# Perceiver kernel: queries stored from ScalarE's queue, the first pair's keys fetched beside the last projection blocks, the negated maxima rounded by ScalarE

## The reference, cut to what matters

```python
# layer 0, cross-attention: 16 heads of 16 channels, all masks true
xn = (x - mean(x)) / sqrt(var(x) + 1e-5)
q = (xn @ Wq + bq)          # (2, 256, 256)
k = (ctx @ Wk + bk)         # (2, 4096, 256)
v = (ctx @ Wv + bv)
p = softmax(q_h @ k_h.T / sqrt(16))   # per head h
x = x + concat_h(p @ v_h) @ Wo + bo
```

## Time and profile before

| | us |
|---|---|
| runs, median of 3 | 1144.29 (1140.45 to 1147.24) |
| the profiled execution | 1140.79 |
| its span, first to last instruction | 1139.5 |
| projection, to the barrier | 0 to 140.7 |
| first attention | 140.7 to about 534 |
| the rest (not touched) | about 534 to 1139.5 |

### The profile page before, as it was taken

One profiled execution on the slowest core, in us unless ns is written; L12 is line 12 of the kernel. 1 busy time (PEld: TensorE's weight loads), 2 busy tenths in 40 slices (PEclk: granted clock), 3 DMA queues, 4 the chain that ended last, 5 costly groups with the idle time before them and its releaser, 6 DMA issues. The chain is left out here.

```text
span 1139.5 us, 20829 instructions
## 1 busy us (share of the span) xinstructions
PE 955.4 (84%) x7631; PEld 599.1 (53%) x7648; DVE 848.7 (74%) x1772; ACT 651.4 (57%) x1067; POOL 295.7 (26%) x313
## 2 busy tenths in 40 slices
PE   5997859999999999996989989248878888987586
PEld 5876724444444444443668875134555556634354
DVE  5775789999899999942567876998878785265447
ACT  3442307788788888874445425059999997202121
POOL 1000088899600000000112521006373631000010
PEclk9999958999999999997789996567799989997797
DMA  5867642222222222200312228002363136830000
GB/s 178 310 234 272 239 134 61 76 79 83 76 74 79 81 79 77 74 1 12 103 49 77 71 61 221 1 1 60 97 181 87 56 98 209 203 110 1 1 1 19
DMA packets 99322, 111.83 MB, mean 98 GB/s; under 512 B 26658, under 2 KB 75731, under 8 KB 99219
## 3 DMA queue, kind: packets, MB, share of 16 engines
q1 hardware_dynamic: 96802, 109.50, 32.0%
q10 hardware_dynamic: 2416, 0.99, 0.4%
HBM read 80.95 MB, written 29.43 MB: 97 GB/s over the span
## 5 line engine op out<-in xcount | busy, mean ns | idle before, releaser
L835 ACT ACTIVATE pT<-bank 128x512 f32<-128x512 f32 x512 | 278.5, 597 | 93.2 <-PE bank L752 71.9
L857 DVE TENSOR_REDUCE rmax<-bank 128x2 f32<-128x1024 f32 x256 | 307.3, 1223 | 26.4 <-PE bank L720 25.4
L764 PE MATMUL bank<-pT,V 128*17 128x256 f32 x2048 | 161.1, 387 | 4.7 <-ACT oT L841 4.5
L1679 PE MATMUL bank<-K1s,qs 97*128 97x512 f32 x256 | 116.7, 558 | 54.7 <-ACT below L1788 36.7
L752 PEld LDWEIGHTS bank<-qs,ks 49*128 49x128 f32 x1024 | 77.7, 186 | 112.4 <-ACT pT L835 98.9
L1943 POOL TENSOR_TENSOR total<-total,work 128x1024 f32<-128x1024 f32 x40 | 94.8, 2378 | 159.0 <-ACT work L1797 158.1
L752 PE MATMUL bank<-qs,ks 49*128 49x256 f32 x1024 | 130.0, 332 | 2.3 <-ACT pT L835 0.5
L720 PE MATMUL bank<-ks,qs 49*128 49x512 f32 x512 | 110.6, 427 | 16.2 <-DMA ks<-k_parts_d 9.0
L1679 PEld LDWEIGHTS bank<-K1s,qs 97*128 97x128 f32 x256 | 54.8, 227 | 69.8 <-ACT below L1788 38.0
L1849 DVE MAX8 cand<-work 128x8 f32<-128x128 f32 x384 | 76.4, 278 | 0.0
L764 PEld LDWEIGHTS bank<-pT,V 128*17 128x17 f32 x2048 | 34.5, 95 | 63.2 <-ACT pT L835 44.7
(11 more groups left out here) (452 smaller groups left out, 1841.6 us busy)
## 6 DMA issues: line engine op xcount, KB each, us to landing
k_parts_d<-kparts SPq DMA_DIRECT2D x48, 512.0 KB
ks<-k_parts_d SPq DMA_DIRECT2D x381, 64.0 KB, 2.2
K1s<-k_parts_d SPq DMA_DIRECT2D x96, 128.0 KB
cn<-in_ctx SPq DMA_DIRECT2D x32, 384.0 KB, 4.0
cx<-in_ctx SPq DMA_DIRECT2D x16, 384.0 KB, 5.0
w<-in_L_ffn_w SPq DMA_DIRECT2D x32, 128.0 KB, 2.7
w2e<-in_L_ffn_w SPq DMA_DIRECT2D x16, 128.0 KB, 2.4
W<-in_L_xattn_W SPq DMA_DIRECT2D x2, 1024.0 KB, 8.3
```

The source lines that it names most:

```text
L764: t = pe.matmul(bank[32 * c:32 * c + VW, 7, a * S:(a + 1) * S], V[:, b * NCH + 4 * g + c, h, :], pT[:, (at + 2 * (c // 2) + a) % 8, c % 2 ...
L835: p_made.up(act.activation(pT[:, at % 8, :], bank[:, 4 + at % 3, :], ACT.Exp))
L857: max_read.up(dve.tensor_reduce(rmax[p % 2][:, :, qt, c], bank[:, b0:b0 + 2, :], AX.X, ALU.max))
L1679: m = pe.matmul(bank[:, b0 + c, :], qs1[0:NROW1, b * H1 + h, q], K1s[h][0:NROW1, keys], start=True, stop=(what == "new"))
```

## The change

Three edits.

1. **Queries stored from ScalarE's queue.** The twelve stores leave `keys_sync`. `keys_scalar` issues three after the last key part of block 8, three after block 9, and two after each of blocks 10, 11 and 12.
2. **The first pair's keys and queries are fetched in the projection.** A third key buffer `kf` and the query buffers `qs` are allocated before the projection: `kf` where `Ap` lies later, `qs` behind `Bp`. ScalarE's program issues the rows of ones after block 10, the keys of the pair's first head after block 13 (three DMAs of 256 KB) and of its second head after block 14, then waits for the query stores and issues the queries of pairs 0 and 1 (four DMAs of 49 KB). After the barrier SyncE starts with the keys of pair 1 and goes on with pair 2 without a wait; ScalarE issues two rows of ones for each of the two buffers `ks`. Pair 0 computes from `kf`. GpSimd's powers wait, before they write `Ap` and `Bp`, until pair 0 is scored.
3. **The negated maxima are rounded by ScalarE.** `copy_rows` moves from `heads_vector` to `heads_scalar`, with its own count `rows_read`; for pair `p+1` it stands before unit 25 of pair `p`, between the two `Exp` of step 12, for pair 0 before all units. Waits for a max bank go through `read_by`, which picks `rows_read` or `max_read`.

```diff
     V = sb("V", [P, NB * NCH, H0, VW])
+    HALF_P = P // 2
+    below = spot[0]
+    spot[0] = LATER + 2 * 4 * LB * 32 * 4
+    qs = [sb(f"qs{j}", [P, S], F32R) for j in range(3)]
+    spot[0] = END - 2 * S2 * 4
+    kf = sb("kf", [P, S2], F32R)
+    spot[0] = below
...
-            if n in (8, 9):
-                store_queries(n - 8)
...
+    def store_queries(mt, b, k):
+        act.wait_ge(*q_split.at(2 * mt + 2))
+        h0 = b * H0 + mt * (P // D0)
+        r0, kp, qp = STACK[k]
+        q_stored.up(act.dma_start(q_stack_d[h0:h0 + P // D0, r0:r0 + D0, :], qparts[:, mt, qp, b * S:(b + 1) * S].bitcast(F32)), 16)
+
+    def load_queries(queue, p):
+        for a in range(2):
+            query_in[p % 3].up(queue.dma_start(qs[p % 3][HALF_P * a:HALF_P * a + NROW, :].bitcast(F32), q_stack_d[2 * p + a]), 16)
+
+    def key_ones(queue, keys, done):
+        for a in range(2):
+            r = HALF_P * a + MAX_ROW
+            done.up(queue.dma_start(keys[r:r + 1, :].rearrange("p (a n) -> p a n", a=8).bitcast(F32),
+                                    ones[0:1, :].rearrange("p (a n) -> p a n", a=1).to_broadcast([1, 8, 512])), 16)
+
+    def load_first_keys(a):
+        for r0, kp, qp in STACK:
+            kf_in.up(act.dma_start(kf[HALF_P * a + r0:HALF_P * a + r0 + D0, :].bitcast(F32),
+                                   k_parts_d[a * D0:(a + 1) * D0, kp, :]), 16)
...
# keys_scalar, at the end of each block n
+            if n in (8, 9):
+                for k in range(NSTK):
+                    store_queries(0, n - 8, k)
+            if n in (10, 11, 12):
+                for b in range(2):
+                    store_queries(1, b, n - 10)
+            if n == 10:
+                key_ones(act, kf, kf_in)
+            if n in (13, 14):
+                load_first_keys(n - 13)
+            if n == 14:
+                act.wait_ge(*q_stored.at(16 * (1 + 4 * NSTK)))
+                load_queries(act, 0)
+                load_queries(act, 1)
...
+    def read_by(at):
+        rows = sum(what[1] == "rows" for what in passing[:at + 1])
+        return rows_read.at(rows) if passing[at][1] == "rows" else max_read.at(at + 1 - rows)
+
+    def keys_of(p):
+        return ks[p % 2] if p else kf
...
# powers_pool, before the first write of Ap
+        pool.wait_ge(*st_made.at(UNITS))
...
     def heads_sync():
+        for p in range(1, NP_):
             if p >= 3:
                 sp.wait_ge(*st_made.at(UNITS * (p - 2)))
             if p >= 2:
+                load_queries(sp, p)
             for q in range(4):
+                if p >= 3:
+                    sp.wait_ge(*st_made.at(UNITS * (p - 2) + 8 * (q + 1)))
+                for a in range(2):
+                    load_key_parts(sp, p, a, q)
...
# heads_tensor: max_step, turn_rows, add_quarters
-                pe.wait_ge(*max_read.at(at - 1))
+                pe.wait_ge(*read_by(at - 2))
# scores
-                pe.wait_ge(*max_read.at(place[p, "rows"] + 1))
+                pe.wait_ge(*rows_read.at(p + 1))
...
     def heads_scalar():
+        for j in (1, 0):
+            key_ones(act, ks[j], kones_in[j])
+
+        def copy_rows(p):
+            at = place[p, "rows"]
+            act.wait_ge(*max_made.at(at + 1))
             for a in range(2):
                 r = HALF_P * a + MAX_ROW
+                t = act.copy(qs[p % 3][r:r + 1, :], bank[r:r + 1, 2 * (at % 2), 0:S])
+            rows_read.up(t)
...
+        copy_rows(0)
         for p in range(NP_):
             for u in range(UNITS):
+                if u == 2 * (16 - LEAD) + 3 and p + 1 < NP_:
+                    copy_rows(p + 1)
                 exps(p, u)
...
# heads_vector: copy_rows is gone, "rows" is passed over
```

More of the change, by code:

```diff
@@ L300, in build @@
     V = sb("V", [P, NB * NCH, H0, VW])
+    HALF_P = P // 2
[5 more added lines that the diff above has]
+    spot[0] = below
+    kf_in = flag("kf_in")
+    query_in = [flag(f"query_in{j}") for j in range(3)]
     phase_begins()
@@ L542, in build @@
     phase_ends()
[L545 removed]
+    NP_ = NH // 2
     G = 8
@@ L567, in build @@
     key_in = [[flag(f"key_in{j}{q}") for q in range(4)] for j in range(2)]
-    query_in = [flag(f"query_in{j}") for j in range(3)]
-    max_made, max_read, nmax_made = (flag(n) for n in ("max_made", "max_read", "nmax_made"))
+    max_made, max_read, rows_read, nmax_made = (flag(n) for n in ("max_made", "max_read", "rows_read", "nmax_made"))
     st_made, p_made, pv_made, oT_copied, den_made, o_done = (flag(n) for n in (
@@ L751, in scores @@
                     rows = slice(HALF_P * a, HALF_P * a + NROW)
-                    t = pe.matmul(bank[:, 4 + (at + a) % 3, c * S:(c + 1) * S], ks[p % 2][rows, k0:k0 + P],
+                    t = pe.matmul(bank[:, 4 + (at + a) % 3, c * S:(c + 1) * S], keys_of(p)[rows, k0:k0 + P],
                                   qs[p % 3][rows, :], start=True, stop=True)
@@ L858, in max_step @@
             if u == 15:
-                dve.wait_ge(*max_read.at(at + 1))
+                dve.wait_ge(*read_by(at))
                 nmax_made.up(dve.tensor_reduce(nmax[:, :, :].rearrange("p t (a m) -> p a t m", a=2)[:, :, :, MAX_ROW],
                                                rmax[p % 2][:, :, :, :], AX.X, ALU.max, negate=True))
-        def copy_rows(p):
-            at = place[p, "rows"]
-            dve.wait_ge(*max_made.at(at + 1))
-            for a in range(2):
-                r = HALF_P * a + MAX_ROW
-                t = dve.tensor_copy(qs[p % 3][r:r + 1, :], bank[r:r + 1, 2 * (at % 2), 0:S])
-            max_read.up(t)
         def take_sums(p):
@@ L877, in divide @@
             pairs = slice(b * H0 // 2, (b + 1) * H0 // 2)
-            dve.wait_ge(*max_read.at(place[pairs.stop - 1, "sums"] + 1))
+            dve.wait_ge(*read_by(place[pairs.stop - 1, "sums"]))
             if b == 0:
@@ L911, in heads_vector @@
                     add_batch(0)
-            else:
+            elif u != "rows":
                 max_step(p, u)
```

55 lines of the change are left out of this document (13 added, 42 removed).

## The result

Six runs of the changed kernel have the median 1157.01 us (1154.49 to 1160.3), the kernel before 1140.81 us on the same chip: ratio 1.0132, 95% interval 1.0101 to 1.0162. The forecast of 1141.3 us was wrong: 16 us slower instead of 3 us faster. The profiled execution took 1157.37 us, with a span of 1156.1 against 1139.5.

The account below looks back on a forecast made before the run. It took TensorE as the projection's bound except for waits, and TensorE with the score matmul and `Exp` ring just below in attention. Terms -4.6 - 4.0 + 2.0 + 3.6 = -3.0 us gave 1141.3 us, range 1133.5 to 1149.

Parts of the forecast that it names:

- query stores: Projection, blocks 9 and 10: context loads issued earlier, TensorE's waits of 5.6 us shrink, gain 4.6 us.
- first keys, behind the barrier: After the barrier: first max matmul no longer waits for key loads, 4.0 us less, bounds 0 and 4.1.
- barrier later for the fetch: End of projection: early loads delay the last stores and move the barrier by 2.0 us, bounds 0 and 4.
- rounding, 15 pairs: First attention: copies on ScalarE cost net 0.24 us a pair, 15 times, 3.6 us more.
- remaining waits: Projection: TensorE's waits for context loads left after moving the query stores, put at 1.0 us, between 0 and 5.6.
- rival D: Projection: context loads land as late as before because the DMA bytes are the same; 1145.9 us, chance 0.17.
- 0.99 MB at 346 / 0.89 = 389 GB/s are 2.5 us, of which about 0.5 us fits between the stores: Before the barrier: DMA time of the loads after block 14, moving the barrier by 2.0 us.
- The far bound of 4 us: Barrier's largest delay: loads to 16 partitions at half the rate, none fitting between the stores.
- with 256 columns ... 0.27 us, both 0.54: Step 12 on ScalarE: time of the two rounding copies, interpolated from 128-partition copies of 128 and 512 columns.
- the same ring: First attention: score matmul, `Exp`, next score matmul; a late `Exp` delays step 14's score matmul, by 0.30 us.
- C: First attention: copies between `Exp`s cost 0.78 us per pair, 11.7 in all; 1149.4 us, chance 0.13.
- Rival B: First attention: the rounding copies hide in ScalarE's slack; 1136.8 us, chance 0.25.

Follow-up runs that it names:

- e2: Kernel before with query stores and rounding on ScalarE, without the early fetch of keys and queries: 1149.86 us, ratio 1.0065.
- e5: Kernel before with only the query stores moved to ScalarE's queue: 1139.02 us, ratio 0.9976.
- e3: Changed kernel with the rounding copies one unit earlier, ahead of unit 24, where ScalarE is idle: 1144.97 us, ratio 1.0027.
- e11: Changed kernel with 24 early 64 KB key loads from SyncE after blocks 10 to 13, rounding back on VectorE: 1137.50 us, ratio 0.9944.
- e10: Changed kernel with rounding back on VectorE and two unread 128x256 float32 copies in its place on ScalarE: 1141.70 us, run once.
- e8: Changed kernel with 24 early 64 KB key loads from SyncE after blocks 10 to 13, rounding on ScalarE ahead of unit 24: 1137.14 us, ratio 0.9967.
- e6: Kernel before with only the rounding moved to ScalarE, ahead of unit 25: 1153.01 us, ratio 1.0073.
- e9: Changed kernel with the rounding written as an Identity activation instead of a copy: 1154.03 us, run once.
- e7: Kernel before with query stores on ScalarE's queue and rounding on ScalarE ahead of unit 24, no early fetch: 1139.35 us, ratio 0.9974.
- e1: Changed kernel with the rounding back on VectorE: 1142.22 us, ratio 0.9998.
- e4: Changed kernel with each 256 KB key load of pair 0 split into four of 64 KB, from ScalarE: 1154.72 us, ratio 1.0109.
- e12: Changed kernel run again, nothing changed: 1155.69 us, ratio 1.0116 to the kernel before.

## Why the prediction was wrong

Its terms against what they measure (barrier and first matmul split by e2 and the marker of block 1, the pairs by the markers):

| term | forecast | measured |
|---|---|---|
| start of the execution, before all that was changed | none | +0.75 |
| query stores | -4.6 | -3.9 |
| first keys, behind the barrier | -4.0 | -4.0 |
| barrier later for the fetch | +2.0 | +8.2 |
| rounding, 15 pairs | +3.6 | +9.3 |
| clock low for longer | none | +1.6 |
| end of the attention, last `oT` to barrier | none | -0.9 |
| rest, not touched | none | +5.6 |
| sum | -3.0 | +16.6 |

**Right: the query stores.** The remaining waits were put at 1.0 us and are 1.75, so 3.8 us of waits are gone; rival D, with both waits kept, is refuted by them, here and in e5. ScalarE's three issues took 2.78 and 3.10 us against an idle 2.58 and did no harm. The Trainium skill, *DMA: Bandwidth & Descriptors*, "Issuing engines are not separate DMA queues", says that another issuer saves issue time alone; the trace agrees, since that time (4.75 and 5.13 us) was the cause of the waits.

**Right: the head start.** 1.98 us from the barrier to the first matmul, forecast 2.0 to 2.1.

**Wrong: "0.99 MB at 346 / 0.89 = 389 GB/s are 2.5 us, of which about 0.5 us fits between the stores".** This step gave the barrier +2.0 us; the fetch costs +8.2. Three things failed in it. The rate was that of the stores; the loads with rows of 16 KB ran at 216 GB/s, and the stores beside them at 253 instead of 388 (changed kernel against e2). The loads after block 13 were held to fit the 3.5 us of idle DMA time; at 216 GB/s their 786 KB take 3.6 us, the stores beside them need longer too, and from 120 to 136 us the engines are 99% busy. And the fetch was followed only to SyncE's last store. Who waits for the stores on the way wasn't asked: block 15's key parts go into block 13's buffer, and ScalarE's wait for it makes 1.85 us of the 8.2. The far bound of 4 us failed as well. It had the loads' rate about right (half of 389), but 0.99 MB at that rate are 5.1 us and not 4, and it left the slower stores and ScalarE out.

**Wrong in size: "with 256 columns ... 0.27 us, both 0.54".** This step gave +3.6 us; the rounding costs +9.3. The mechanism was right: the second `Exp` comes late, step 14's score matmul waits for it, nothing catches up, and VectorE's freedom is worth nothing (e3, e11). The inserted time was interpolated between copies with 128 partitions that overlap their neighbours, and the copies with one partition don't. With 0.89 in place of 0.54 the same ring gives 0.65 a pair; 0.63 is measured. Even the kind of copy interpolated has 0.61 instead of 0.54 (e10). The Trainium skill, *ScalarE: Activation LUTs*, "What ACT_TABLE_LOAD costs", gives 186 ns + 0.833 ns a column; the estimate from it is 399 ns for 256 columns, and the trace agrees for 128 partitions (402); its overlap of 93 ns is met there about (two take 0.70 us instead of 0.80) and not at all by the 1x256 copies.
Of the rivals C came nearest: 11.7 us for the rounding, on 0.78 a pair, measured 0.62. It took the cost from the copy `oT`, which differs in shape, so part of that is luck. Rival B fell; its argument against, that the copies stand behind the gap and not in it, is what e3 turned into the remedy.

**Missed: the clock.** TensorE's idle time at the barrier is followed by a clock of 0.50, and how long that lasts behind the first max matmul differs by up to 15 us between executions with the same work there. It gave 1.6 us of the loss, and 2.7 of the 3.7 us that e5 loses between the barrier and the last `oT`. At the attention's end it gave some back: the clock fell 8.4 us ahead of the last barrier in the kernel before (526.4 us) and 4.2 ahead in the changed one (541.6).

**Open: the rest.** The last 5.6 us lie in code that the change doesn't touch. Count the microseconds there whose granted clock is under 0.75, in each profiled execution:

```
        e5    e10   e8    e3    e6    e9    e2    e7    e1    before e11   e4    e12   changed
low us  178   185   187   188   188   191   198   198   198   198    202   212   212   219
rest    599.5 598.4 598.8 601.2 602.7 606.7 605.9 605.9 603.3 604.7  604.6 609.9 608.3 610.3
```

The rest goes with the low clock, and the changed kernel is at the upper end twice. Why its falls of the clock last longer there is not shown: kernels with the same code in the rest lie anywhere between. A link to the rounding can't be excluded. The six executions with pairs of about 22.6 us (changed, e12, e2, e4, e6, e9) have a rest of 602.7 to 610.3 us, mean 607.3; the eight others have 598.4 to 605.9, mean 602.0. The two groups overlap, and no run was made to part them. So the net 9.6 us of stores, fetch, head start and rounding have a shown cause. The remaining 7 us, the start, the clock and the rest, are measured but not explained. The medians leave the same gap: the queries -0.24% (e5), the rounding +0.73% (e6), the fetch +0.22% (e1 against e5), together +0.71%, but the whole +1.16 and +1.32%. Each of these has an interval of 0.2 to 0.5% on either side, so part of the gap can be noise. What makes the clock fall again near the last pair of e2 and e6, and not of the changed kernel with the same rounding, is open too.

## What to carry to other kernels

A transfer moved ahead of a barrier must be priced at the rate of its own shape, and followed to everyone who waits for the transfers that it slows: the stores at the barrier, and the engine that needs their buffer back. Issue it from the queue that has time, and early enough that the idle share of several blocks takes it; short rows were part of the version that worked (e8), but by themselves gained nothing (e4). An instruction inserted into a ring of two engines costs its inserted time less the slack; measure that time start to start with its own shape, and look for the place where the engine waits anyway, because one position earlier can make it free. And before a stage is compared between two traces, look at a marker ahead of everything that was changed: here it was up to 1.4 us apart with the same code.

## What the runs showed of the hardware

- Copies of 1x256 by ScalarE from PSUM to a float32r tile took 365 ns (`Identity` 376) and overlapped neither each other nor an `Exp`; float32 copies of 128x256 from SBUF to SBUF took 402 ns and overlapped on both sides.
- Loads of 256 KB in 16 KB rows to 16 partitions ran at 216 GB/s of full share, and the stores beside them at 253 instead of 388 GB/s. Loads in 4 KB rows ran at 288 GB/s over a window whose stores ran at 374, and at 252 where no store ran.
- After the same barrier with the same work behind it, TensorE's clock stayed at its lower level for 31 to 46 us; a step bound by TensorE took 2.14 us instead of 1.22.
- Identical code of some 600 us took 598.4 to 610.3 us in 14 profiled executions of 13 kernels, with 178 to 219 us of it at a lower granted clock.
